# One maximum per head: a 1,024-column reduction read as two of 512, with a semaphore step for each bank

## The reference, cut to what matters

```python
q = _layernorm(q, qn_scale, qn_bias)
k = _layernorm(k, kn_scale, kn_bias)
qg = q.reshape(b, g, hg, n, d)
dots = jnp.einsum('bghqd,bgkd->bghqk', qg, k) * scale
attn = jax.nn.softmax(dots, axis=-1)
out = jnp.einsum('bghqk,bgkd->bghqd', attn, v)
out = out.transpose(0, 3, 1, 2, 4).reshape(b, n, g * hg * d)
return out @ Wout
```

## Time and profile before

| What | Value |
|---|---|
| median of 3 executions | 918.61 us |
| lowest and highest | 915.94 and 921.15 us |
| the profiled execution's own time | 922.55 us |
| its span in the trace | 920.8 us |
| TensorE matmuls busy | 849.5 us, 92% of the span |
| VectorE busy | 631.1 us, 69% |
| GpSimd busy | 542.3 us, 59% |
| ScalarE busy | 456.3 us, 50% |
| mean granted TensorE clock | 0.965 of full speed |

### The profile page before, as it was taken

The page is one execution under the profiler, slowest core; times in us unless marked ns, Lnnn a source line. Parts: engine busy times, 40 slices in busy tenths (PEclk is TensorE's granted clock), DMA queues, the critical chain, the costliest instruction groups (busy, mean ns, idle before and its releaser), DMA issues. The chain is left out here.

```text
span 920.8 us, 13439 instructions
## 1 busy us (share of the span) xinstructions
PE 849.5 (92%) x4860; PEld 448.2 (49%) x4860; DVE 631.1 (69%) x1072; ACT 456.3 (50%) x822; POOL 542.3 (59%) x319
## 2 busy tenths in 40 slices
PE   2797899999999999979799999999999964999998
PEld 2454444444444444544344444444444422567675
DVE  6877677777777777378767777777777637155772
ACT  2464455555555555555455555555555532444522
POOL 3323588868886888602368768876888753046510
PEclk9899899999999999999899999999999995899989
DMA  6000000000000000000000000000000001100001
GB/s 163 1 0 1 1 1 1 1 1 2 1 1 1 2 1 1 1 1 1 0 1 2 2 1 1 1 1 1 2 2 1 1 4 47 47 1 1 1 1 46
DMA packets 49596, 7.98 MB, mean 9 GB/s; under 512 B 42486, under 2 KB 47994, under 8 KB 49530
## 3 DMA queue, kind: packets, MB, share of 16 engines
q1 hardware_dynamic: 48666, 6.99, 4.8%
q10 hardware_dynamic: 864, 0.13, 0.1%
HBM read 5.92 MB, written 1.05 MB: 8 GB/s over the span
## 5 line engine op out<-in xcount | busy, mean ns | idle before, releaser
L977 DVE TENSOR_REDUCE part<-psum 128x2 f32<-128x1024 f32 x256 | 313.3, 1224 | 139.3 <-PE psum L511 139.2
L399 POOL TENSOR_TENSOR space<-space 128x1024 f32<-128x1024 f32 x160 | 380.6, 2378 | 40.3 <-ACT space L752 22.8
L752 ACT ACTIVATE space<-psum 128x512 f32<-128x512 f32 x512 | 264.5, 602 | 157.9 <-PE psum L531 155.0
L546 PE MATMUL psum<-space,vb 128*64 128x512 f32 x1024 | 248.6, 607 | 0.0
L511 PE MATMUL psum<-kh,qh 64*128 64x512 f32 x512 | 129.4, 502 | 14.1 <-DVE part L977 13.7
L404 POOL TENSOR_TENSOR space<-space 128x1024 f32<-128x1024 f32 x30 | 71.6, 2387 | 106.6 <-DVE space L991 106.6
L511 PEld LDWEIGHTS psum<-kh,qh 64*128 64x128 f32 x512 | 48.4, 186 | 154.9 <-DVE part L977 119.5
L546 PEld LDWEIGHTS psum<-space,vb 128*64 128x64 f32 x1024 | 62.5, 136 | 107.4 <-issue 102.0
L531 PE MATMUL psum<-qh,kh 64*128 64x512 f32 x512 | 103.6, 401 | 0.0
L531 PE MATMUL psum<-ql,kh 64*128 64x512 f32 x512 | 102.3, 396 | 0.0
L531 PE MATMUL psum<-qh,kl 64*128 64x512 f32 x512 | 101.9, 394 | 0.0
(11 more groups left out here) (160 smaller groups left out, 875.0 us busy)
## 6 DMA issues: line engine op xcount, KB each, us to landing
ql<-nmx SPq DMA_DIRECT2D x256, 0.5 KB, 2.0
w1s<-in_L_ffn_W SPq DMA_DIRECT2D x4, 256.0 KB, 2.7
w2s<-in_L_ffn_W SPq DMA_DIRECT2D x4, 256.0 KB
out<-x SPq DMA_DIRECT2D x4, 256.0 KB, 2.7
x<-in_L_attn_x SPq DMA_DIRECT2D x2, 256.0 KB, 4.5
wproj<-in_L_attn_Wq SPq DMA_DIRECT2D x1, 512.0 KB, 6.6
x<-in_L_attn_x SPq DMA_DIRECT2D x1, 512.0 KB, 8.1
wout<-in_L_attn_Wout SPq DMA_DIRECT2D x1, 512.0 KB, 7.0
```

The lines of the kernel that those rows point to most:

```text
L399: pool.tensor_tensor(to, pt[0] if u == 1 else to, pt[u], ALU.add)\
L546: last = pe.matmul(outp[rows(h), :], vb[:, place(m)[1], kt, :], pt[kt][:, h, :], start=(kt == 0), stop=(kt == TILES - 1))
L752: act.activation(pt[kt][:, h, :], key_scores[kt % 2][h], ACT.Exp).then_inc(exp_made, 1)
L977: dve.tensor_reduce(to[:, half, :], scores.rearrange("p (h k) -> p h k", h=2), AX_X, ALU.max, negate=True)\
```

## The change

VectorE reads each unit in two reductions of 512 columns, one for each head and bank, both raising `part_made` by one. The count for a whole unit is therefore two. The matmul of head 0 of the next unit waits for the first of the two, the matmul of head 1 for the second. `scored` is still raised once for each unit, by its last matmul. The values that `turn_keys` and the small reduction wait for are doubled to match.

```diff
@@ turn_keys
                 elif b:
-                    pe.wait_ge(part_made, 8 * SLOTS * b)
+                    pe.wait_ge(part_made, 16 * SLOTS * b)
@@ unit_scores
-                if n or k:
-                    pe.wait_ge(part_made, 8 * n + k)
                 for h in range(2):
+                    if n or k:
+                        pe.wait_ge(part_made, 2 * (8 * n + k) - 1 + h)
                     last = pe.matmul(scores[:, h * 512:(h + 1) * 512],
                                      qh[rows(h), PAIRS * g + hp, at * QB + t * P:at * QB + (t + 1) * P],
                                      kh[rows(h), g, half * 512:(half + 1) * 512], start=True, stop=True)
@@ largest
                 dve.wait_ge(scored, 8 * n + k + 1)
-                dve.tensor_reduce(to[:, half, :], scores.rearrange("p (h k) -> p h k", h=2), AX_X, ALU.max, negate=True)\
-                   .then_inc(part_made, 1)
+                for h in range(2):
+                    dve.tensor_reduce(to[:, half, h:h + 1], scores[:, h * 512:(h + 1) * 512], AX_X, ALU.max, negate=True).then_inc(part_made, 1)
                 if half:
                     if k == 1 and n >= 2:
                         dve.wait_ge(max_placed[n % 2], 16 * 8 * (n // 2))
-                    dve.wait_ge(part_made, 8 * n + k + 1)
+                    dve.wait_ge(part_made, 2 * (8 * n + k) + 2)
                     dve.tensor_reduce(nmx[n % 2][:, pair, :], to.rearrange("p f h -> p h f"), AX_X, ALU.min).then_inc(max_made, 1)
```

## The result

The changed kernel took 927.43 us in the median of four executions (927.29 to 929.27); the kernel before took 918.0 on the same occasion (four executions, 915.94 to 921.15). The ratio is 1.0096, 95% interval 1.0067 to 1.0124: **slower by about 1%**, more than the half per cent that can be told from no change. The profiled execution took 929.27 us with a span of 927.5.

The account below looks back on a forecast made before the run. TensorE was taken to set the pace, waiting about 0.15 us a phase before unit B. 118 x 0.017 = 2.0 us plus 1.4 us in `produce` gave +3.4, 922.0 us against the median 918.61; range 914.5 to 929.5 us.

Parts of the forecast that it names:

- the first rival: Before the values: head 1's part behind the release stays as long as the pair's; +0.07 us a phase, 928.3 us; chance 0.16.
- the forecast's own sum: Attention phases 2.0 us and `produce` 1.4 us, together +3.4 us; 922.0 us against the median.
- nothing can be seen: Whole kernel: 0.4% slower, below the 0.5% (4.6 us) that a measurement can tell from no change.
- What bounds the kernel: Attention phases: TensorE sets the pace and waits for the maximum once a phase, before unit B, about 0.15 us.
- VectorE's price: Reductions of a unit: the pair takes 1.295 us against 1.225, so head 1's maximum comes 0.07 us later.
- the second rival: VectorE between the two reductions: nothing overlaps, pair 1.38 us, 0.10 us a phase longer, 933.5 us; chance 0.12.
- Head 0 goes early, and gains nothing by itself: Unit B on TensorE: head 0's matmul, released at 254.345, stops waiting, but takes nothing off head 1's time once released.
- One thing is saved, a weight load: Unit B on TensorE: only head 1's load stays exposed, saving 0.055 us; each phase gets about 0.017 us longer.
- Outside the phases: In `produce`: 10 units of each batch charged the full 0.07 us, 1.4 us; nothing if the idle stretch takes it up.
- The tell-tales: Expected trace signs: head 1 1.97 us after unit A, unit A not waiting, slot 18.54 us, VectorE busy 40 us more.
- the forecast's own last test: Forecast wrong if a slot moves over 0.15 us either way, or head 0's matmul starts together with head 1's.
- The third rival, a shrinking wait: Before unit B: head 1's load hidden too, pair as long as the old reduction, values 0.10 us sooner; 906.8 us; chance 0.12.

Follow-up runs that it names:

- the runs with only one unit split: Changed kernel with only unit A, or only unit B, read in two reductions: ratios 1.0105 and 1.0066; only B, every reduction raising part_made by one: 1.0003.
- the run with 256 columns: Changed kernel with head 1's reduction reading 256 of its 512 columns, leaving keys out of its maximum: 892.9 us, ratio 0.9709.

## Why the prediction was right or wrong

The measured time lies in the range, on the slower side, because the range had been drawn to take in the first rival, and not because the forecast's own sum was right: it had 3.4 us, and the medians of the same occasion differ by 9.4 (6.2 to 11.4 by the interval). The forecast of "nothing can be seen" did not come true; the result is the first rival's, 928.3 us, "the load is not saved".

- **What bounds the kernel: right, and undersized.** TensorE waits once in a phase, before unit B, and not before unit A (the runs with only one unit split). The wait was put at 0.15 us; the run with 256 columns shows 0.205: unit B then starts 1.71 us after unit A, where I had taken 1.75 from the spacing of the pairs, and the values follow the matmuls 0.02 sooner.
- **VectorE's price: right.** Forecast 1.295 us for the pair and 0.605 from start to start; recorded 1.29. The bound of 1.38 (the second rival) did not occur. The Trainium skill's rule (VectorE: DVE Perf Modes, The DRAIN you can't avoid), read strictly, would have given it; 1.29 for two operations of 0.68 and 0.69 us disagrees with that reading. The same section adds that a next operation that is not held starts earlier, and the 1.29 agrees with that.
- **Head 0 goes early, and gains nothing by itself: right.** It starts 1.72 us after unit A without a wait.
- **"One thing is saved, a weight load": wrong, the step that failed.** This term made 0.017 us of a phase out of 0.07. The values follow 0.43 us behind head 1's load alone, as they followed 0.42 behind the pair, and with both loads behind the release the slot is the same. The mistake was to read 0.42 - 0.32 = 0.10 us as the price of two loads, half each, from a phase of another kind. What a second load costs behind a first was nowhere to be seen in it; one exposed load and two leave the same 0.42 to 0.43, so the 0.10 fits the price of exposed loading as such, however many. With the term taken out, the sum is 118 x 0.065 = 7.7 us in the phases. From the first unit to the last the trace has 671.9 us (60.63 to 732.51) instead of 664.7 (59.93 to 724.62), 7.2 more, but that is no clean check: the first 20 us of batch 0's phases (from 89.7 and 90.9 us) ran at a granted clock of 0.67 and 0.93 in the profiled execution before, and of 0.74 and 1.00 in the one after. The slots of the earlier trace rows and of the window above, at 1.00 both, are the cleaner measure.
- **Outside the phases: about half of the 1.4 us**, by the one round of `produce` read above, in which the idle stretch took up the other half.
- **The tell-tales:** head 1 at 1.97 after unit A (measured 1.95), unit A without a wait (right), a slot of 18.54 (measured 18.74), VectorE's busy time up by 40 us (measured 16; the time that two records share had been counted twice). By the forecast's own last test it was wrong: a slot moved by 0.26 us, more than 0.15.
- **The third rival, a shrinking wait, did not occur**, for the reason given: what waits behind the unit needs the second half. The Trainium skill's advice (Perfetto Trace Analysis, Optimizing Scalar/DVE Operations) to break up operations where VectorE makes another engine pause did not help here, because the pause ends with the last piece.

What stays open is why 0.43 us lie between head 1's load and the values in every run, whatever went ahead. The Trainium skill (TensorEngine Tiling (Array Packing), Key Properties) says that a change of tiling mode drains the engine. That `project_out` ahead of unit B cost 0.08 us a slot fits it, but no run here separates the drain from the load. Open too is what the compiled program does in the instruction on VectorE's queue, and whether its time or only its place ahead of the reduction makes the delay: the two always came together.

## What to carry to other kernels

Handing a result over in pieces helps only if the consumer can go on with a piece. Here the work behind both matmuls needed both, so the early piece was worth nothing and the later end of the last one cost 0.065 us in each phase. Ask for each split: what waits behind the last piece, and does that piece come sooner or later than the whole did? Where a wait sits on a tight loop between two engines, look at the semaphores that its instruction handles beside the one that counts, and at the queue's own instructions in the trace: moving one wait to a neighbour with time to spare gave 0.8%, which none of the edits to the reduction itself did without leaving keys out.

## What the runs showed of the hardware

- A VectorE reduction that waits for two semaphores started 0.07 us later behind its last condition than one that waits for one (0.61 and 0.54 us behind the unit), though the second had long been met. With the second wait the trace has a semaphore instruction of 21 ns on VectorE's queue (126 before, 127 with the wait moved), and the delay moved with it.
- A reduction that raises its semaphore by two started 0.02 to 0.07 us later than one that raises it by one (0.63 and 0.61 instead of 0.61 and 0.54), 0.6% of the time of this kernel. Here too the queue has such an instruction, ahead of all 256 reductions, of 21 to 50 ns. Two reductions that raise it by one each did not show this (0.61 and 0.54).
- On TensorE a second wait, already met, ahead of the second matmul of a pair cost nothing (slots of 18.47 in both).
- Two reductions of 512 columns from PSUM back to back took 1.29 us, one of 1,024 took 1.225; the second of the pair starts inside the recorded time of the first.
- The values' first load started 0.42 to 0.43 us behind the last exposed weight load of a 64-row pair, whether one load of the pair was exposed or both, and 0.32 behind a pair whose loads were done early.
